# Attention with adapter and int8 layer: the steps behind attention leave PSUM through ScalarE in place of VectorE

## What is computed

```
cond = x @ W[id] + b[id]                       # one weight matrix per batch
q, k, v = split(cond @ w_qkv.T)                # 16 heads of 32
s = q k^T / sqrt(32) - slope*|i-j|             # causal
p = 0.5*(1 + s*rsqrt(1 + s*s));  p /= sum(p) + eps
x1 = x + (p v) @ w_out.T
h  = relu(x1 @ W1[lid] + b1[lid])              # adapter, 512 -> 128
y  = x1 + h @ W2[lid] + b2[lid]                # 128 -> 512
z  = (y - mean(y)) * rsqrt(var(y) + 1e-5) * gamma[lid] + beta[lid]
out = x1 + int8(z / xs) @ w8.T * xs * ws + bias    # xs = max|z| / 127 over both batches
```

## Time and profile before

| | us |
|---|---|
| median of the three runs | 2297.26 |
| lowest and highest | 2292.51, 2299.26 |
| span of the profiled execution | 2294.5 |
| joining group in it (1086.5 to 1407.3) | 320.8 |
| ending group (1877.1 to 2162.4) | 285.3 |
| a plain group (1407.3 to 1642.6) | 235.3 |

### The profile page before, as it was taken

One profiled execution on the slowest core, in us unless ns is written; L12 is line 12 of the kernel. 1 busy time (PEld: TensorE's weight loads), 2 busy tenths in 40 slices (PEclk: granted clock), 3 DMA queues, 4 the chain that ended last, 5 costly groups with the idle time before them and its releaser, 6 DMA issues.

```text
span 2294.5 us, 30517 instructions
## 1 busy us (share of the span) xinstructions
PE 1763.6 (77%) x10128; PEld 873.0 (38%) x10128; DVE 1917.8 (84%) x2114; ACT 1686.5 (74%) x1938; POOL 1901.6 (83%) x1038
## 2 busy tenths in 40 slices
PE   5678877777787788998888876777687777786864
PEld 4555332323332345664444333333332333342331
DVE  4358888888889899898898898888889898899758
ACT  0247897889789888888656567889889888767413
POOL 2147998999989998898888888999989998898648
PEclk9899988888888899999999998888889898898879
DMA  5411111111111022202222221111111031121137
GB/s 177 140 48 43 48 34 30 47 40 30 34 39 48 20 80 60 69 18 81 76 75 80 65 57 30 43 44 27 38 39 48 20 85 39 39 65 47 51 123 239
DMA packets 126618, 138.64 MB, mean 60 GB/s; under 512 B 27868, under 2 KB 78044, under 8 KB 126044
## 3 DMA queue, kind: packets, MB, share of 16 engines
q1 hardware_dynamic: 126460, 136.64, 21.1%
HBM read 54.02 MB, written 22.80 MB: 33 GB/s over the span
## 4 chain that ended last, share of the span: by engine, by line
PE 24%; POOL 24%; DVE 19%; issue 14%; ACT 13%; SPq 2%; DMA 2%; DVEq 0%; POOLq 0%; ACTq 0%
POOL yb L626 18%; DVE gb L990 6%; ACT yb L677 6%; DVE gb L1049 5%; ACT yb L679 5%; PE sc L835 4%; PE ov L815 4%; PE it L748 3%; PE dn L815 3%; ACT gb L669 3%; PE it L731 3%; PE it L755 3%; POOL gb L605 2%; PE it L735 2%; POOL oT L662 2%
## 5 line engine op out<-in xcount | busy, mean ns | idle before, releaser
L626 POOL TENSOR_TENSOR yb<-yb 128x1024 f32<-128x1024 f32 (+3 forms) x640 | 1468.5, 2301 | 310.2 <-DVE gb L1049 296.0
L677 ACT ACTIVATE yb<-sc 128x1024 f32<-128x1024 f32 (+3 forms) x640 | 567.1, 886 | 398.8 <-PE sc L835 310.6
L990 DVE TENSOR_TENSOR gb<-gb,yb 128x1024 f32<-128x1024 f32 (+3 forms) x640 | 817.2, 1277 | 36.7 <-POOL yb L626 35.3
L1049 DVE TENSOR_TENSOR gb<-sc,yb 128x1024 f32<-128x1024 f32 (+3 forms) x640 | 676.4, 1057 | 150.3 <-ACT yb L679 147.2
L835 PE MATMUL sc<-qmv,kst 128*128 128x512 f32 (+3 forms) x1280 | 473.7, 458 | 333.7 <-DVE gb L1049 317.4
L679 ACT ACTIVATE yb<-yb 128x1024 f32<-128x1024 f32 (+3 forms) x640 | 595.1, 930 | 20.3
L669 ACT ACTIVATE gb<-gb 128x1024 f32<-128x1024 f32 (+3 forms) x640 | 584.1, 913 | 0.8 <-DVE gb L1049 0.8
L835 PEld LDWEIGHTS sc<-qmv,kst 128*128 128x128 f32 x1280 | 216.3, 206 | 699.8 <-DVE gb L1049 520.0
L815 PE MATMUL ov<-gb,vv 128*32 128x512 f32 (+3 forms) x2560 | 337.8, 603 | 37.2 <-DVE den L1086 15.3
L815 PE MATMUL dn<-gb,ones 128*32 128x512 f32 (+3 forms) x2560 | 326.4, 584 | 0.0
L731 PE MATMUL it<-hT,wT 128*128 128x512 f32 x496 | 254.6, 639 | 5.8 <-DVE area L928 1.8
(11 more groups left out here) (109 smaller groups left out, 1020.4 us busy)
## 6 DMA issues: line engine op xcount, KB each, us to landing
qmv<-stage SPq DMA_DIRECT2D x384, 64.0 KB
kst<-stage SPq DMA_DIRECT2D x384, 64.0 KB
area<-in_x_dram SPq DMA_DIRECT2D x58, 256.0 KB, 2.8
out_dram<-oT SPq DMA_DIRECT2D x32, 256.0 KB, 3.5
den<-rec_d SPq DMA_DIRECT2D x31, 256.0 KB
wT<-wT_d SPq DMA_DIRECT2D x7, 768.0 KB, 4.4
x_d<-area SPq DMA_DIRECT2D x16, 256.0 KB, 2.6
z_d<-area SPq DMA_DIRECT2D x16, 256.0 KB, 3.1
```

What stands on the lines that cost most here:

```text
L626: pool.tensor_tensor(y, y, y, ALU.mult).then_inc(s_y2, 1)
L677: act.activation(y, sc[:, k % SLOTS, :, q0_of(g, k):], ACT.Square).then_inc(s_s2, 1)
L990: dve.tensor_tensor(t, t, yview(k)[:, :, q0:], ALU.add).then_inc(s_num, 1)
L1049: dve.tensor_tensor(gview(k)[:, :, q0:], sc[:, k % SLOTS, :, q0:], yview(k)[:, :, q0:], ALU.mult).then_inc(s_g, 1)
```

## The change

Three evacuations of each tile behind attention move from VectorE to ScalarE: the transposed copy (`rt`, a Copy), bias and relu (`a`, a Relu with b1 as a per-partition operand), and gamma/beta (`zt`, four Identity instructions with a scale and a bias for each partition). They count on a semaphore of their own, `s_evac_act`; TensorE and SP look up for each item which engine empties it (`ranks`, `emptied`). VectorE keeps the largest absolute value, in a function `largest` of its own, which it calls behind the scoring of a later pair. GpSimd normalises as y*rstd + shift in place of (y-mean)*rstd, with shift = -mean*rstd made by one more instruction of one column.

```
+ON_ACT = ("rt", "a", "zt")
...
+                    pool.wait_ge(s_rstd[a], 2 * m + 1)
+                    pool.tensor_scalar(shift[:, a:a + 1], mv[:, a, 0:1], rstd[:, a:a + 1], -1.0,
+                                       ALU.mult, ALU.mult).then_inc(s_rstd[a], 1)
+                    pool.wait_ge(s_rstd[a], 2 * m + 2)
+                    pool.tensor_scalar(res[a], res[a], rstd[:, a:a + 1], shift[:, a:a + 1],
+                                       ALU.mult, ALU.add).then_inc(s_u[a], 1)
-                    pool.wait_ge(s_rstd[a], m + 1)
-                    pool.tensor_scalar(res[a], res[a], mv[:, a, 0:1], rstd[:, a:a + 1],
-                                       ALU.subtract, ALU.mult).then_inc(s_u[a], 1)
...
+            def after(b, job, item, z_before):
+                what, j = job.name
+                a, m = place(b, j)
+                bank = it[:, item % BANKS] if item < REST else end_bank(item)
+                feat = bank.rearrange("p (k n) -> p k n", k=KC)
+                act.wait_ge(s_item, item + 1)
+                if what == "rt":
+                    if m:
+                        act.wait_ge(s_zst[a], 16 * m)
+                        act.wait_ge(s_amax, z_before)
+                    act.activation(resT[a], feat, ACT.Copy).then_inc(s_evac_act, 1)
+                elif what == "a":
+                    act.wait_ge(s_bw, 16 * 7 * (b + 1))
+                    act.activation(hid[a], bank[:, 0:P], ACT.Relu, bias=b1c[:, 0:1]).then_inc(s_evac_act, 1)
+                elif what == "zt":
+                    for k in range(KC):
+                        r = act.activation(resT[a][:, k, :], feat[:, k], ACT.Identity, scale=gam[:, k:k + 1],
+                                           bias=bet[:, k:k + 1])
+                    r.then_inc(s_evac_act, 1)
...
                     if k >= NUM_LAG or g is not opening:
                         one_plus_g_squared(G, g, k - NUM_LAG)
+                    for job in after_pair.get(k, []):
+                        d = b if g is ending else b - 1
+                        after(d, job, bases[0] + job.index, zs_before(d, job.name[1]))
...
+            def emptied(i, of, dve_base, act_base):
+                if i < 0:
+                    pe.wait_ge(s_evac, dve_base + i + 1)
+                elif of[i][0] == "dve":
+                    pe.wait_ge(s_evac, dve_base + of[i][1])
+                else:
+                    pe.wait_ge(s_evac_act, act_base + of[i][1])
...
-                            pe.wait_ge(s_evac, base + item - BANKS + 1)
+                            emptied(item - BANKS, g.ranks, dve_base, act_base)
...
-                    dve.tensor_copy(resT[a], feat).then_inc(s_evac, 1)
-                    dve.tensor_scalar(hid[a], src[:, 0:P], b1c[:, 0:1], 0.0, ALU.add, ALU.max).then_inc(s_evac, 1)
...
-                    for k in range(KC):
-                        r = dve.tensor_scalar(resT[a][:, k, :], feat[:, k], gam[:, k:k + 1],
-                                              bet[:, k:k + 1], ALU.mult, ALU.add)
-                    r.then_inc(s_evac, 1)
-                    dve.wait_ge(s_evac, i + 1)
-                    dve.tensor_reduce(amax[:, b * KB + c:b * KB + c + 1], resT[a].rearrange("p k n -> p (k n)"), AX.X,
-                                      ALU.max, apply_absolute_value=True).then_inc(s_amax, 1)
+            def largest(b, j, done):
+                a, _ = place(b, j)
+                dve.wait_ge(s_evac_act, done)
+                dve.tensor_reduce(amax[:, b * KB + j:b * KB + j + 1], resT[a].rearrange("p k n -> p (k n)"), AX.X,
+                                  ALU.max, apply_absolute_value=True).then_inc(s_amax, 1)
...
                         numerator(G, g, k - NUM_LAG)
+                    while reduced and reduced[0][0] < k:
+                        largest(*reduced.pop(0)[1:])
```

145 lines of the change are left out of this document (90 added, 55 removed).

## The result

The changed kernel takes 2281.86 us in the median of its runs (the kernel before, measured beside it: 2295.72). The ratio is 0.9945, with a 95% interval from 0.9932 to 0.9958: faster by about 12.6 us, or 0.55%; the two medians by themselves lie 13.9 us apart. One of the 14 runs took 4017.16 us, is slow and stays out of the ratio. The forecast was 2276 us, 20.2 us less in its sum. The profiled execution has a span of 2284.0 us.

The account below looks back on a forecast made before the run. VectorE was taken to hold the others back, GpSimd to bound after the change; joining -16.8, ending -5.2 and last block +1.8 sum to -20.2 us, a span of 2274.3; plus 2.8 gives 2277, named 2276, range 2250 to 2300.

Parts of the forecast that it names:

- VectorE's relief: Copy, gamma/beta and relu leave VectorE: 2.26 us a tile, 36.2 us in joining, 22.6 in the ending group.
- ScalarE's price: Moved steps cost ScalarE 1.97 us a tile, upper end 2.49; joining's ScalarE becomes 241.3 us, still least loaded.
- GpSimd's price: Shift adds 0.66 us a tile, pass stays 2.08; GpSimd has 282.7 us in joining, 252.1 in ending, and bounds.
- Joining: Joining group, 16 tiles: GpSimd's 282.7 us at a packing of 0.93 gives 304.0 us, 16.8 less.
- Rival (a): GpSimd's pass falls to 1.24 us: joining 26 less, ending 14 less, last block -3.2; 2254 us. Chance 0.25.
- Ending: Ending group, 10 tiles: 252.1/0.93 + 9 = 280.1 us, 5.2 less.
- the hole: Ending group: VectorE waits 6.3 us for TensorE's projection behind the division, then 2.7 more; 9 us set aside as untouched.
- Rival (b): GpSimd's waits for VectorE become waits on TensorE: joining 317.6, ending 292 taken as unchanged; total -1, 2296 us. Chance 0.15.
- Rival (c): ScalarE empties banks late, behind three full-width instructions: 52 edges at 1 us, 2329 us, slower. Chance 0.12.
- Last block: Last 6 tiles, behind the ending group: GpSimd ends 4.0 us later, the block 1.8 us longer.
- the 0.935: Last 28 pairs of joining: VectorE busy 97.2 of 103.9 us; upper end of the packing taken for GpSimd.

Follow-up runs that it names:

- e2: Changed kernel with GpSimd's old subtract-and-multiply pass and no shift instruction, the three evacuations still on ScalarE: 2286.16 us, ratio 0.995 to the kernel before.
- e1: Kernel before with only GpSimd's normalisation changed (shift, multiply-and-add), all evacuations on VectorE: 2296.57 us, ratio 1.0009 to the kernel before.
- e8: Changed kernel with only copy and relu on ScalarE; gamma/beta and the reduction back on VectorE: 2296.91 us, ratio 1.0009 to the kernel before.
- e11: Changed kernel with ScalarE emptying a bank ahead of its pair's first Square instead of behind the third: 2309.1 us, ratio 1.0058 to the kernel before.
- e12: Changed kernel, ending group emptied ahead of the first Square, int8 loads held until VectorE's last small step behind the reduction: 2280.61 us, ratio 0.9924.
- e9: Changed kernel with only gamma/beta on ScalarE in the ending group, all three evacuations there in joining and last block: 2282.66 us, ratio 0.993.

## Why the prediction was right or wrong

The time came within 6 us of the forecast, and it moved the way that was forecast. The mechanism behind it failed, and terms that were off in opposite ways made the sum come out near: that part is luck.

**VectorE's relief: right.** 36.2 us were forecast for joining; it is 33.4 in one pair of executions and 32.1 in the other (285.0 to 252.9).

**ScalarE's price: at the upper end.** A gamma/beta instruction takes 452 ns, not 275. Four of them take 1.50 us in a row (2039.37), the copy 0.58, bias with relu 0.35: 2.4 us a tile for the 1.97 taken and the upper end of 2.49. The row of 380 ns for 256 elements was the better guide to a 128-column piece than the line through wider ones. The Trainium skill's formula (ScalarE: Activation LUTs, What ACT_TABLE_LOAD costs) gave an estimated 1.54 us for the four, and the trace agrees with 1.50. It changed nothing that can be seen in joining, where ScalarE had the room. No table was reloaded: the trace of after has the two loads of before.

**GpSimd's price: wrong, and with it the premise of the forecast.** The forecast said "I take 2.08" for the pass and "It takes VectorE's place as the bound", with 282.7 us in joining at a packing of 0.93. Both steps failed. GpSimd measured 260.2 us: the pass takes 0.77 us in the last block and 1.18 on the average in the groups, the shift 0.26 in the last block and 0.42 in the groups (forecast 0.66 with its wait). Even the lower bound of 1.24 us, from an addition with two tensor inputs, was no bound. And even with the pass at 2.08 us (e2) GpSimd is busy for 269.3 of 307.1 us, 0.88 and not 0.93, so it is no bound there either. The Trainium skill's best case of 769 ns (GPSIMD Engine Reference, Elementwise - side-by-side cycle accounting), which the forecast set aside because the pass of before stood at 2.08, is what multiply-and-add reaches.

**Joining: the right size for a wrong reason.** 304.0 us were forecast, 305.6 and 309.0 came. But e2 has the same joining group (307.1) with the dear pass and e1 shows nothing for the cheap one. The first part of the prediction read from the earlier trace rows that VectorE holds the others back, and that fits better: taking work off VectorE is what e2 has and e1 has not. TensorE's waits for VectorE's `area` fell from 23.7 to 5.0 us there, and 10.8 us of waits for ScalarE came in their place; between the means of the two executions each, all its idle time fell by 8.5 us and its busy time by 3.7, with the clock. That the gain is the move's is shown; how it comes about inside the group is not, since e8 has nearly the same waits and no gain.

**Rival (a): its price was near, its time wrong.** It named the cheap pass and asked for 26 us less in joining, 295 us, and for 271 in ending. Its 1.24 us lie near the 1.18 of the groups and above the 0.77 of the last block. TensorE was to be packed as in the closing group, 0.90; it reached 260.9/305.6 = 0.85. No engine is full in joining: TensorE is idle for about 45 us in every kernel with this order and this assignment, and its waits are spread over VectorE, ScalarE and GpSimd.

**Ending: wrong sign.** The step "252.1/0.93 + 9 = 280.1" gave -5.2 us; measured over the same stretch +8.1 and +4.7, and +4.5 in the mean up to the division. The 9 us set aside for the hole were right (6.93 and 2.74 us of wait stand in the changed kernel too, at 2121.60 and 2125.03). What failed is treating the ending group as a matter of the fullest engine: VectorE lost 17.5 us of work there and GpSimd 2.5, and the group grew. TensorE's waits for `area` rose from 9.9 us for VectorE to 4.4 for VectorE and 14.7 for ScalarE, against 7 us less for the scores; its idle time rose by 2.7 us, its busy time by 1.9 to 5.4. But e1, with all of it on VectorE, is 5.3 us longer too (idle 1.7, busy 3.6), so ScalarE's waits are not the whole cause, and what is stays open. Rival (b)'s own arithmetic had 292 for this group, which it then took as unchanged.

**Rival (c): its waits came, its loss did not.** It decided "from 0.4 us an edge", an edge being a place where TensorE needs what ScalarE empties. Over 32 edges of joining TensorE waits 10.8 us for ScalarE, 0.34 each, over 20 of the ending group 14.7, 0.74 each: 0.49 on the average, above its threshold, and still the kernel is faster. The threshold left out the waits for VectorE that go: 18.7 us in joining against 10.8 that come, but 5.5 in the ending group against 14.7. The forecast's view that ScalarE's own wait for an item "by itself costs nothing" was not strained: ScalarE's idle time ahead of its three new kinds of instruction is 6.6 us over all head groups. e11, which puts that wait ahead of Square, has 61.6 us of it in joining and is 26 to 30 us longer there.

**Last block: wrong sign from the same term.** +1.8 us became -7.5. With the pass at 0.77 us GpSimd keeps up with VectorE's statistics (a normalisation every 1.75 us, 2206.71 to 2204.96, not 2.71), and gamma/beta run on ScalarE beside it. e1, e2 and e8 show that this needs both the cheap pass and gamma/beta off VectorE.

**The int8 layer: not in the sum.** The prediction let the changed kernel's end be the same. It costs 2.6 us, 0.8 of them because the reduction starts later behind the maxima; e12 shows that the start of the loads costs 1.6 to 2.1 (69.9 us against 72.0 and 71.5).

In sum: the measured gain (12.6 us by the ratio) is six tenths of the forecast. Joining gave 12.2 of 16.8, and the ending group took 4.5 where 5.2 were to come: 14.3 us short. The last block gave 7.5 where it was to take 1.8, which made good 9.3 of them, and the int8 layer took 2.6 again. Two slips in the prediction weigh little: its sum is 2277 and it named 2276 without a reason, and the 0.935 that it calls the best packing in the two groups is over 28 pairs, while over pairs 52 to 60 of the ending group VectorE was busy for 32.1 of 32.5 us.

## What to carry to other kernels

Ask of a moved evacuation who gives the bank back and how late, stage by stage: the same move shortened one stage by 12 us and did not shorten another. Place it by trying: behind the last instruction of a pair it was worth 12 us in joining, ahead of the last it was worth nothing, and ahead of the first it cost 16. When a change has two parts, run each alone and look at every stage: the part that looked harmless here (e1) lengthened a stage by 5 us, where the other part had an explanation of its own that fitted. In a profile of one execution, split a stage into TensorE's idle and busy time before believing a difference, and don't build a kernel out of the best stage of each variant: e9 and e12 were such, and each repaired place gave most of its gain back a few pairs later. When two short steps run one behind the other at the end, look for what their new timing starts: here a transfer.

## What the runs showed of the hardware

- On GpSimd, one pass over 128x512 float32 with two per-partition operands takes 2.08 us as subtract-and-multiply (line 619 of before) and 0.77 us as multiply-and-add (line 646 of after), in the last block. The two forms differ in the operations and also in one operand (mean and rstd against rstd and shift, each one value a partition); which of the two decides was not tried apart.
- Inside the head groups the same two forms take 2.31 and 1.18 us on the average, with the same 2.08 and 0.77 us as their medians, and up to 3.16 and 1.83; what delays some of them is not tested.
- A reduction over the partitions on GpSimd starts 5.5 to 5.8 us behind GpSimd's own last instruction even when its operand is ready earlier (2212.21 for a start at 2214.20). Where that last instruction was 10.6 us back (e1, e8), it starts 0.26 us behind its operand. The next ordinary instruction comes 6.8 to 7.1 us behind its end, and 8.1 to 9.4 us where SP's first loads of the int8 layer start within 0.4 us behind its start. What fills these gaps no run here shows.
- TensorE's clock enters as a term of its own: the same 1410 products of the joining group took 259.6 us busy at a granted 0.97 and 275.6 at 0.93.
